# Inverse blocks joined on 64 rows, and end-scaled keys formed in their own slot: a delta-rule kernel

## The reference, cut to what matters

```
def step(S, inp):
    qt, kt, vt, gt, bt = inp
    S = S * jnp.exp(gt)[..., None, None]
    pred = jnp.einsum('bhk,bhkv->bhv', kt, S)
    u = (vt - pred) * bt[..., None]
    S = S + jnp.einsum('bhk,bhv->bhkv', kt, u)
    o = jnp.einsum('bhk,bhkv->bhv', qt, S)
    return (S, o)
```

## Time and profile before

| | us |
|---|---|
| time, median of 3 runs (5453.8 to 5462.22) | 5457.68 |
| the profiled execution, its own time | 5472.21 |
| its span, first to last instruction | 5470.4 |
| TensorE matmul busy in the span | 5025.4 (92%) |
| TensorE weight load busy | 4314.4 (79%) |
| VectorE busy | 3880.1 (71%) |
| ScalarE busy | 3128.9 (57%) |
| mean granted TensorE clock | 0.957 |

### The profile page before, as it was taken

One profiled execution on the slowest core, in us unless ns is written; L12 is line 12 of the kernel. 1 busy time (PEld: TensorE's weight loads), 2 busy tenths in 40 slices (PEclk: granted clock), 3 DMA queues, 4 the chain that ended last, 5 costly groups with the idle time before them and its releaser, 6 DMA issues. The chain is left out here.

```text
span 5470.4 us, 100611 instructions
## 1 busy us (share of the span) xinstructions
PE 5025.4 (92%) x33232; PEld 4314.4 (79%) x33232; DVE 3880.1 (71%) x6564; ACT 3128.9 (57%) x10211; POOL 1084.8 (20%) x868
## 2 busy tenths in 40 slices
PE   5999948999999999999969999399999999999999
PEld 3577737888888888888845777288888888888888
DVE  6746887777777777777741588777777677777776
ACT  1144436767676676767611444366666666666665
POOL 0000002223222222322200000033222223232222
PEclk9999979999999999999979999699999999999999
DMA  1023222222222222222101233222222222222221
GB/s 50 24 91 116 97 87 82 70 65 71 67 73 63 70 70 65 72 66 73 51 25 36 99 109 113 70 77 66 69 69 64 70 65 70 68 65 68 60 73 54
DMA packets 410442, 384.28 MB, mean 70 GB/s; under 512 B 232776, under 2 KB 307832, under 8 KB 409486
## 3 DMA queue, kind: packets, MB, share of 16 engines
q1 hardware_dynamic: 409934, 377.51, 22.3%
HBM read 278.74 MB, written 98.66 MB: 69 GB/s over the span
## 5 line engine op out<-in xcount | busy, mean ns | idle before, releaser
L1076 DVE SCALAR_TENSOR_TENSOR conv_l<-mix_l,taps_l,conv_l 128x512 f32<-128x512 f32 x1152 | 995.0, 864 | 375.5 <-ACT conv_l L923 308.4
L738 PE MATMUL pj_l<-x_high,w_high_l 128*128 128x512 f32 x1280 | 586.1, 458 | 210.8 <-ACT w_high_l L931 157.5
L1259 POOL TENSOR_TENSOR fac_l<-den_l,powers 128x4 f32<-128x4 f32 x256 | 254.6, 1007 | 1957.6 <-DVE den_l L1174 1956.7
L738 PE MATMUL pj_l<-x_high,w_low_l 128*128 128x512 f32 x1280 | 518.1, 405 | 0.0
L738 PE MATMUL pj_l<-x_low,w_high_l 128*128 128x512 f32 x1280 | 518.0, 405 | 0.0
L895 PE MATMUL gb_l<-wo_l,gT_l 128*128 128x256 f32 x2048 | 482.0, 384 | 0.0
L738 PEld LDWEIGHTS pj_l<-x_high,w_high_l 128*128 128x128 f32 x1280 | 245.7, 192 | 273.2 <-ACT w_high_l L931 157.8
L1237 POOL TENSOR_TENSOR kqd_l<-kq_l,rows_l 128x1024 f32<-128x1024 f32 x192 | 453.1, 2382 | 0.0
L394 PE MATMUL pk_l<-x_high,wf_high_l 128*128 128x512 f32 x1024 | 426.6, 417 | 21.0 <-DVE wf_low_l L480 21.0
L1041 ACT ACTIVATE Z_l<-gb_l 128x128 f32<-128x128 f32 x1024 | 266.7, 290 | 296.0 <-PE gb_l L886 295.9
L895 PEld LDWEIGHTS gb_l<-wo_l,gT_l 128*128 128x128 f32 x2048 | 371.4, 190 | 72.8 <-ACT Z_l L1041 31.6
(11 more groups left out here) (183 smaller groups left out, 11856.4 us busy)
## 6 DMA issues: line engine op xcount, KB each, us to landing
rows_l<-rows_dram SPq DMA_DIRECT2D x128, 1024.0 KB, 5.7
k_dram<-kT_l SPq DMA_DIRECT2D x128, 256.0 KB, 2.0
kk_dram<-key_kkS_l SPq DMA_DIRECT2D x128, 256.0 KB, 2.1
kq_l<-k_dram SPq DMA_DIRECT2D x128, 256.0 KB, 3.3
kkS_l<-kk_dram SPq DMA_DIRECT2D x128, 256.0 KB, 5.8
w_raw_l<-in_wx SPq DMA_DIRECT2D x32, 640.0 KB
t_dram<-lane_t_l SPq DMA_DIRECT2D x6, 1536.0 KB, 7.0
key_taps_l<-in_ktaps SPq DMA_DIRECT2D x32, 256.0 KB, 3.6
```

Of the source, the lines that this page charges most:

```text
L738: ins = nc.tensor.matmul(pj_bank(c, t), wt[:, k, t, :], xt[:, k, :, at], start=(k == 0 and n == 0), stop=(k == KD - 1 and n == 2))
L1076: ins = nc.vector.scalar_tensor_tensor(out, mix[:, t, :, i:i + P], wt(i), out, ALU.mult, ALU.add)
L1259: nc.gpsimd.tensor_tensor(fac[:, g, :], den[:, g, :], m.powers[:, 1, :], ALU.pow).then_inc(fac_ok[g], 1)
```

## The change

It does two things in `delta_attention`, and adapts what feeds them.

1. The 32 to 64 step works on 64 rows. L797's successor (L811) takes only 64 columns of `ap` as stationary operand and gives 64 rows; L807's (L822) is a 64x64 product. VectorE no longer subtracts: two instructions on 32 rows each, over both groups (L1176), write the negated product into a new tile `W` of 64 rows. Eight transposes of `W` (L834) give 64 columns each in place of 128. X gets its diagonal blocks 2 and 3 by DMA (`load_diagonal`, after `y` of the slot) and the rest by three ScalarE copies over both groups (`copy_right` 32 rows, `copy_left` 64 rows, `copy_corner`). The masked product of keys is formed in four instructions, of the parts that are read. SyncE issues 8 small loads per slot where it issued 6. TensorE transposes the next keys after fill(1) and not before it; it waits for `W` ahead of the last matmul of fill(2). In the PSUM tile `gb` the index of kind and group change places, so L861 (before: L840) now waits for the last corner of X.
2. `ke` of a slot is formed in that slot, after ScalarE's first copies to `Z`, and not at all for c=3, where nothing reads it.

```diff
-                    for g in range(GROUPS):
-                        copy_z(g, it, slice(0, P), z32_mm)
+                    for g in range(GROUPS):
+                        copy_z(g, it, slice(0, HALF), z32_mm)
+                    if c < CHUNKS - 1:
+                        scaled_keys(h, c)
                     if not last:
                         square_keys(nh, ncn, False)
                         copy_mix(nh, ncn, 1, False)
                         copy_mix(nh, ncn, 2, False)
-                    for g in range(GROUPS):
-                        copy_x(g, it)
+                    copy_right(it)
                     for g in range(GROUPS):
                         copy_z(g, it, slice(HALF, P), z64_mm)
+                    copy_left(it)
                     if not last:
                         silu_conv(nh, ncn, 0)
...
                     if not last:
                         scaled_values(nh, ncn)
-                        scaled_keys(nh, ncn)
...
                         for b in range(BATCH):
-                            ins = nc.tensor.matmul(gb[:, g, 0, part(b)], ap[:, c % 2, g, b, 0, :], Te[:, g, b, :],
-                                                   start=True, stop=True)
+                            ins = nc.tensor.matmul(gb[0:HALF, 0, g, part(b)], ap[:, c % 2, g, b, 0, 0:HALF],
+                                                   Te[:, g, b, :], start=True, stop=True)
                         ins.then_inc(z32_mm[g], 1)
+                    fill(1)
+                    pe.wait_ge(xd_in, 32 * (it + 1))
+                    for g in range(GROUPS):
+                        pe.wait_ge(z_cp[g], 2 * it + 1)
                     if not last:
                         keys_token_major(nh, ncn, False)
-                    fill(1)
...
-                            ins = nc.tensor.matmul(gb[:, g, 1, part(b)], Xd[:, g, b, :], Z[:, g, part(b)],
+                            ins = nc.tensor.matmul(gb[0:HALF, 1, g, part(b)], Xd[:, g, b, :], Z[0:HALF, g, part(b)],
                                                    start=True, stop=True)
                         ins.then_inc(dx_mm[g], 1)
-                    fill(2)
-                    for g in range(GROUPS):
-                        pe.wait_ge(tm_up[g], it + 1)
-                        pe.wait_ge(tm_in, 32 * (it + 1))
+                    if not last:
+                        project(nh, ncn, 2, 0, False)
+                        project(nh, ncn, 2, 1, False, (0, 1))
+                    pe.wait_ge(w_blocks_in, 32 * (it + 1))
+                    pe.wait_ge(w_up, 2 * (it + 1))
+                    if not last:
+                        project(nh, ncn, 2, 1, False, (2,))
+                    for g in range(GROUPS):
                         for b in range(BATCH):
-                            ins = nc.tensor.transpose(gb[:, g, 1, bank(b)], Tm[:, g, b, :], eye)
+                            ins = nc.tensor.transpose(gb[:, 1, g, part(b)], W[:, g, b, :], eye[0:HALF, 0:HALF])
...
+                            pe.wait_ge(x_cp, 3 * (it + 1))
                             pe.wait_ge(kqd_ok[g], 3 * h + c)
...
-                        nc.vector.tensor_tensor(blocks(Tm[:, g, :, :], 0), Te[:, g, :, :].rearrange(
-                            "p b (n half) -> p b n half", half=QUAD), change, ALU.subtract).then_inc(tm_up[g], 1)
+                    for n, cols in ((1, slice(0, QUAD)), (0, slice(HALF, HALF + QUAD))):
+                        rows = slice(n * QUAD, (n + 1) * QUAD)
...
+                        nc.vector.tensor_scalar(W[rows, :, :, cols], new, -1.0, None, ALU.mult).then_inc(w_up, 1)
...
+                    if not last:
+                        sp.wait_ge(y_mm[1], 4 * h + c + 1)
+                        load_diagonal(*following(h, c))
```

More of the change, by code:

```diff
@@ L332, in store_blocks @@
                     sp.wait_ge(tt_ok, k + 1)
[L333 to L336, removed]
+                    sp.dma_start(m.tt_dram[L][h:h + n].rearrange("h q p i c -> (q p) h (i c)"),
+                                 Tt[QUAD:, 0:n, :, :].rearrange("p h i c -> p h (i c)")).then_inc(tt_out, 16)
                 def store_products(q):
@@ L616, in delta_attention @@
             "pj_read", "q_silu", "v_silu", "k_sq", "q_sq", "ktok_cp"))
-        z_cp, x_cp, y_cp, o_cp, o_sq = (pair(x) for x in ("z_cp", "x_cp", "y_cp", "o_cp", "o_sq"))
+        z_cp, y_cp, o_cp, o_sq = (pair(x) for x in ("z_cp", "y_cp", "o_cp", "o_sq"))
         tap, conved, n2_ok, rn2_ok, bcol_ok, qcol_ok = (sem(x) for x in (
@@ L621, in delta_attention @@
         decay_ok, ap_ok, ke_ok, vn_ok = (sem(x) for x in ("decay_ok", "ap_ok", "ke_ok", "vn_ok"))
-        tm_up, r_ok, s_ok, gate_ok, den_ok, res_ok = (pair(x) for x in (
-            "tm_up", "r_ok", "s_ok", "gate_ok", "den_ok", "res_ok"))
+        r_ok, s_ok, gate_ok, den_ok, res_ok = (pair(x) for x in (
+            "r_ok", "s_ok", "gate_ok", "den_ok", "res_ok"))
         wo_ok, halo_ok, ncol_ok, diag_ok = (sem(x) for x in ("wo_ok", "halo_ok", "ncol_ok", "diag_ok"))
@@ L642, in delta_attention, with odd_columns @@
         part = lambda b: slice(b * HALF, (b + 1) * HALF)
-        def blocks(t, odd):
-            return t.rearrange("p b (n two half) -> p b n two half", two=2, half=QUAD)[:, :, :, odd, :]
+        def odd_columns(t):
+            return t.rearrange("p b (n two half) -> p b n two half", two=2, half=QUAD)[:, :, :, 1, :]
         def pj_bank(c, t):
@@ L674, in load_products @@
                     sp.dma_start(kkS[:, :], m.kk_dram[L][bass.ds(h, 1), c, :, :].squeeze(0)).then_inc(kk_in, 16)
-                def load_blocks(h, c):
[L677 to L690, removed]
@@ L692, in _, with load_diagonal @@
+                def load_diagonal(h, c):
+                    by_b = X[:, :, :].rearrange("p g (b n) -> p g b n", b=BATCH)
+                    for q in (2, 3):
+                        sp.dma_start(by_b[quad(q), :, :, quad(q)], transposed_blocks_of(h, c, q)).then_inc(x_in, 16)
                 load_keys(0, 0)
@@ L725, in _, with project @@
             def _(pe):
-                def project(h, c, t, k, first):
+                def project(h, c, t, k, first, terms=(0, 1, 2)):
                     q = 4 * h + c
-                    if k == 0:
+                    if k == 0 and terms[0] == 0:
                         if c == 0:
@@ L818, in body @@
                         for b in range(BATCH):
[L819 to L820 removed]
+                            ins = nc.tensor.matmul(gb[HALF:, 0, g, part(b)], ap[0:HALF, c % 2, g, b, 0, HALF:],
+                                                   W[:, g, b, 0:HALF], start=True, stop=True)
                         ins.then_inc(z64_mm[g], 1)
                     fill(3)
+                    pe.wait_ge(x_in, 32 * (it + 1))
+                    pe.wait_ge(x_cp, 3 * it + 1)
                     for g in range(GROUPS):
                         pe.wait_ge(z_cp[g], 2 * it + 2)
[L825 removed]
                     if not last:
@@ L829, in body @@
                         for b in range(BATCH):
-                            ins = nc.tensor.matmul(gb[0:HALF, g, 1, part(b)], Z[HALF:, g, part(b)],
+                            ins = nc.tensor.matmul(gb[0:HALF, 0, g, part(b)], Z[HALF:, g, part(b)],
                                                    X[HALF:, g, b * P + HALF:(b + 1) * P], start=True, stop=True)
@@ L839, in body @@
                             for b in range(BATCH):
-                                ins = nc.tensor.matmul(gb[:, g, 0, bank(b)], kqd[:, g, b, 0, :],
+                                ins = nc.tensor.matmul(gb[:, 0, g, bank(b)], kqd[:, g, b, 0, :],
                                                        S[:, c % 2, g, bank(b)], start=True, stop=True)
@@ L1059, in _ @@
                 scaled_values(0, 0)
-                scaled_keys(0, 0)
                 steps(act, body)
@@ L1122, in masked_products @@
                         dve.wait_ge(decay_ok, 2 * q + g + 1)
-                        nc.vector.tensor_tensor(ap[:, c % 2, g, :, 0, :], by4(kkS[:, :]), by4(decay[:, g, :]),
+                        odd = ap[:, c % 2, g, :, 0, 0:HALF].rearrange("p b (n half) -> p b n half", half=QUAD)
+                        nc.vector.tensor_tensor(odd, odd_columns(by4(kkS[:, :])), odd_columns(by4(decay[:, g, :])),
                                                 ALU.mult).then_inc(ap_ok, 1)
+                    for g in range(GROUPS):
+                        nc.vector.tensor_tensor(ap[0:HALF, c % 2, g, :, 0, HALF:], by4(kkS[0:HALF, :])[:, :, HALF:],
+                                                by4(decay[0:HALF, g, :])[:, :, HALF:], ALU.mult).then_inc(ap_ok, 1)
                     dve.wait_ge(kk_mm, q + 1)
@@ L1136, in body @@
                         dve.wait_ge(dx_mm[g], it + 1)
-                        change = gb[:, g, 1, 0:BATCH * HALF].rearrange("p (b n half) -> p b n half", b=BATCH, half=QUAD)
-                        nc.vector.tensor_tensor(blocks(Tm[:, g, :, :], 0), Te[:, g, :, :].rearrange(
```

(6 more changed lines are left out.)

118 lines of the change are left out of this document (70 added, 48 removed).

## The result

The changed kernel takes 5623.3 us, median of 4 runs (5613.6 to 5641.67), beside 5455.74 (5453.09 to 5462.22) for the kernel before: ratio 1.031, 95% interval 1.029 to 1.033. It is slower by 3.1%, and the forecast was 5428. Its profiled execution took 5626.86, its span is 5624.8.

What follows compares the result with a forecast made beforehand. TensorE, busy 92% of the span, was taken as the bound, with ScalarE's chain deciding more. Work gains of 67 us gave 5391; the clock rhythm left 30: 5472.2 - 30 - 14.5 = 5428 us, range 5362 to 5464.

Steps and rivals of the forecast that it cites:

- TensorE's groups: L811 and L822 on TensorE: 0.5 us less each; with 0.3 from the transposes, 1.3 a slot if nothing waits.
- By it the 0.3 would be nothing: W's transposes: if load time goes by columns, their 0.3 us saving vanishes, about 10 us less where TensorE leads.
- ScalarE's chain: ScalarE's summed work lets L760 (now L774) start at +10.25 at best in c=0 to 2, about +9.3 in c=3.
- the 0.35, 0.3, 0.2 and 1.25 taken: Gains in us assumed for slots c=0, 1, 2 and 3: 2.1 a head, 67 over 32 heads.
- VectorE: In c=1 and 2 the convolution ends about +5.8, W at +6.5; TensorE waits 1 us, at no further cost.
- each tenth there would go straight to the end of these slots: In c=1 and 2, if GpSimd's cover of VectorE's convolution were longer, each extra tenth would lengthen the slot.
- The clock, as a rhythm: Clock falls hold layer 0's heads to 119.4 us, gaining nothing; layer 1 gains 30 us.
- The slower rival: Falls at TensorE's new idles before L760 and the transposes, 1.5 to 2.8 us each; 5535 at all 96 slots; chance 0.11.
- Its odds: Falls in the new idles got 0.11, slower overall 0.10; these idles are half as long as ones followed by falls.
- Costed at nothing: SyncE's extra loads, the queued weight loads and L861's wait at no cost; prologue and `key_blocks` under 2 us either way.
- The keys' move: With `ke` out of the tail, every slot's ScalarE work can start at +0.34, as c=0 does.

Runs made afterwards that it cites:

- the idle filled: The changed kernel with seven unread 128x512 matmuls ahead of TensorE's wait for W in slots c=1 and 2: 5481.96 us, ratio 1.006.
- W early: The changed kernel with VectorE's W writes ahead of the last instruction of the first convolution: 5401.58 us, ratio 0.991.
- the fastest kernel: The changed kernel with W written ahead of the first convolution's last instruction and the keys formed at the end of the slot before: 5333.9 us, ratio 0.978.
- join: The 32 to 64 step; run alone as the changed kernel with the keys back at the end of the slot before: 5534.91 us, ratio 1.015.
- the keys alone: The kernel before with only the end-scaled keys moved into their own slot and left out for c=3: 5521.67 us, ratio 1.013.

## Why the prediction was wrong, by its steps

- **TensorE's groups**: right. From start to the next group's start L811 takes 1.07 to 1.20 (medians by slot) and L822 1.07, where L797 and L807 took 1.73 and 1.70. The transposes take 0.63 to the next group's start (1364.84 to 1365.47, with the idle filled) where they took 0.97: 0.3 was taken. The Trainium skill's page "TensorE: Matmul & The Clock Gate", Part 2, step LDWEIGHTS, says that a load's time goes by its columns and not by its rows, and the trace agrees: one load of these transposes takes 142 ns with 128 rows (L815) and 140 with 64 (L834, W early), both of 128 columns. What did not follow is the prediction's "By it the 0.3 would be nothing": the transposes came every 0.11 us and now come every 0.06, so the length of a load did not set their pace.
- **ScalarE's chain**: right wherever W is on time. L774 starts at +10.20 in c=0 (said: +10.25), and at +10.20 in c=1 and 2 with W early. In c=3 it starts at +9.30 with W early, as said, and at +10.03 in the changed kernel of layer 0, since W is late there as well. But the slots gained less than L774 did: with W early 0.22, 0.16, 0.12 and 0.94 (medians of layer 0) for the 0.35, 0.3, 0.2 and 1.25 taken.
- **VectorE**: this step failed. The text said that the convolution "starts 0.7 earlier but still runs under `kqd` and `Sd` to about +5.8", W at +6.5, TensorE waiting 1 us, "the transposes start where L815 did". It ended at +6.45, W at +7.35, the wait was 1.62, the transposes started 1 us behind L815. The durations of the earlier trace rows were moved 0.7 earlier as they stood. They were not the instructions' own: each was as long as GpSimd's instruction beside it made it, and GpSimd's had moved by only 0.09 (`Sd` ended at +5.91). That `Sd` ended at +6.00 and the convolution at +6.55 stood in the same rows, and would have given +6.5 at once. With "each tenth there would go straight to the end of these slots" the text named the price: 0.9 a slot, 58 us in all. And the wait it had at 1 us was the 1.62 that 58 of 64 slots followed with a fall, 150 us more.
- **The clock, as a rhythm**: wrong. No head is held to 119.4. With W early a typical head takes 117.8, with clock 1.00 in c=0 to 2 and 0.98 in c=3, in the fastest kernel 115.7, with 1.00 in all four slots. In the changed kernel heads grew to about 126, and the falls came behind the stops for W.
- **The slower rival** (0.10 for slower) was right in its mechanism, a fall behind the stop before the transposes, and near in its counting: it put the falls at 1.5 to 2.8 each and the turning point at 45 of them; it was 58 of 2.6. It said 5535 for all 96 slots. In part that was luck. It counted on stops of 0.9 and 1 us, and such stops (c=0, before L774, median 1.00) were followed by a fall in one slot of 32; the falls came because the stop for W was longer than it had it. The missing 88 us are mostly W's lateness, 58, which it took as nothing, and the gains of c=1 and 2 that it still counted, 0.5 a head or 16.
- **Its odds** were set on "these idles are half as long as the ones followed by falls". That was so of the 1 us, not of 1.62, and the share of falls rises steeply between the two (24, 37 and 58 of 64 slots at 1.2, 1.35 and 1.7).
- **Costed at nothing**: SyncE's loads stayed so; no wait of TensorE names a DMA of these tiles. The keys' move was costed as a gain of a start at +0.34. It took back about half of the gain of join and early W together: 62 to 68 of some 120 us.

## What to carry to other kernels

When work is moved against another engine's, do not move its durations with it. Ask which of them are its own and which are stretched by a neighbour that stays where it was. An instruction that was hidden behind TensorE's work (here the write of W behind two convolution instructions) becomes the bound when that work shrinks, so check the order of each in-order engine again after every cut on the bounding one. A stop of TensorE of 1.3 to 1.7 us ahead of small products can cost more by the clock than by itself, 2.6 against 0.9 us here; that what comes behind the stop matters is not shown, only that stops as long before other work were followed by few falls or none.

## What the runs showed of the hardware

**VectorE beside GpSimd.** A convolution instruction takes 0.75 us alone. Beside `kqd` and `Sd` each ended about 0.55 us after the end of GpSimd's instruction (less than its own 0.75; no run shows why), whenever it had started: the first took 1.29 when started at +2.35 and 2.10 when started at +1.45, and ended at +3.6 both times. VectorE's L1221, which reads one of its two large inputs from PSUM, runs beside `kqd` at its usual 0.48. The Trainium skill's page "SBUF — State Buffer", section "SBUF: two separate sides", describes this: VectorE instructions with two SBUF inputs and GpSimd's share a pair of ports, as a lock held for a whole instruction. By it an earlier start gains nothing until GpSimd is through, and the trace agrees.

**The clock.** Stops of 1.2 to 1.7 us ahead of the transposes of W were followed by a stretch at 1.2 GHz in 24 to 58 of 64 slots, stops of 0.3 in none. Stops of 1.5 and 1.8 us ahead of L880 were followed by one in 0 and 4 of 32 slots. The stop at a head's end, about 2 us in each, was followed by one that took over 5 us of the next slot in 8 heads of 32 before, in 18 with the keys alone, and in none of the fastest kernel, where 3 had a shorter one. So a stop's length alone does not tell whether a fall follows; what else does is open.
